# A four-stage Flamingo block on one core: output projection and routing by token halves, the first expert shares by a selector product, weights fetched during the attention, and key-query products behind the key tiles

## The reference, cut to what matters

```python
x = x + tanh(g_xattn[0]) * L0_xattn(layernorm(x), ctx)   # x (4, 256, 256), ctx (4, 1601, 128)
x = x + tanh(g_ffn[0])   * L0_ffn(layernorm(x))          # 32 experts of 96, top 8, capacity
x = x + tanh(g_xattn[1]) * L1_xattn(layernorm(x), ctx)   # 16 heads of 128, rms-normed q and k
x = x + tanh(g_ffn[1])   * L1_ffn(layernorm(x))          # 64 experts of 64, top 4, 2 shared
```

## Time and profile before

| | us |
|---|---|
| median of 3 runs | 1975.44 (1975.04 to 1980.54) |
| the profiled execution | 1977.05 |
| its span in the profile | 1974.9 |
| busy: TensorE / VectorE / ScalarE / GpSimd | 1829.2 / 1366.6 / 1162.3 / 336.6 |
| granted TensorE clock, mean over the span | 0.968 of full speed |

### The profile page before, as it was taken

The page is one execution under the profiler, slowest core; times in us unless marked ns, Lnnn a source line. Parts: engine busy times, 40 slices in busy tenths (PEclk is TensorE's granted clock), DMA queues, the critical chain, the costliest instruction groups (busy, mean ns, idle before and its releaser), DMA issues. The chain is left out here.

```text
span 1974.9 us, 31470 instructions
## 1 busy us (share of the span) xinstructions
PE 1829.2 (93%) x9085; PEld 1342.2 (68%) x9087; DVE 1366.6 (69%) x2268; ACT 1162.3 (59%) x1943; POOL 336.6 (17%) x298
## 2 busy tenths in 40 slices
PE   5789898949999889999899998999989998999998
PEld 3444444547888667776677766777667776788887
DVE  8565656245666678877778787878778786666665
ACT  2577666813333567776677767777667774333222
POOL 3010101023444300001000010000100002444442
PEclk9899999969999999999999999999999997999999
DMA  3413223155443200001000010000000001455553
GB/s 93 105 49 73 70 53 77 29 170 127 112 113 85 67 1 0 0 0 34 0 0 0 0 34 0 0 0 0 1 1 0 0 0 38 88 112 112 114 114 82
DMA packets 110127, 96.58 MB, mean 49 GB/s; under 512 B 72836, under 2 KB 94472, under 8 KB 109416
## 3 DMA queue, kind: packets, MB, share of 16 engines
q1 hardware_dynamic: 110056, 95.67, 19.7%
HBM read 73.73 MB, written 1.44 MB: 38 GB/s over the span
## 5 line engine op out<-in xcount | busy, mean ns | idle before, releaser
L902 ACT ACTIVATE s_p<-ps,s_g,s_rk 128x256 f32<-128x256 f32 (+1 forms) x832 | 412.3, 559 | 126.4 <-PE ps L1129 91.5
L1129 PE MATMUL ps<-s_qq,s_ctxT 128*128 (+2 forms) x1248 | 389.6, 425 | 18.4 <-ACT s_p L902 15.7
L423 PE MATMUL ps<-s_xT,s_wgus 128*128 128x512 f32 x1440 | 350.5, 393 | 3.0 <-DVE s_hw L1643 2.6
L423 PEld LDWEIGHTS ps<-s_xT,s_wgus 128*128 128x128 f32 x1440 | 272.2, 189 | 62.1 <-DVE s_hw L1643 3.4
L1129 PEld LDWEIGHTS ps<-s_qq,s_ctxT 128*128 128x128 f32 (+1 forms) x1248 | 231.7, 187 | 106.7 <-issue 47.2
L1129 PE MATMUL ps<-s_ps,s_ctx 128*128 128x512 f32 x960 | 276.5, 398 | 0.1
L817 ACT ACTIVATE s_p<-ps,s_bsm 128x1024 f32<-128x1024 f32 x208 | 219.1, 1111 | 96.1 <-PE ps L1010 85.0
L1763 DVE TENSOR_TENSOR s_dsum<-s_dsum,s_p 128x512 f32<-128x512 f32 (+1 forms) x352 | 242.2, 688 | 30.4 <-ACT s_p L902 19.6
L1772 DVE TENSOR_TENSOR s_ps<-s_p,s_ps 128x512 fp32r<-128x512 f32 x320 | 220.1, 688 | 13.2 <-ACT s_ps L908 9.8
L1129 PEld LDWEIGHTS ps<-s_ps,s_ctx 128*128 128x128 f32 x960 | 182.2, 190 | 46.7 <-DVE s_ps L1772 1.8
L1645 DVE TENSOR_TENSOR s_hs<-s_hw,s_hs 128x512 fp32r<-128x512 f32 x120 | 138.7, 1156 | 82.3 <-ACT s_hs L346 82.3
(11 more groups left out here) (253 smaller groups left out, 2128.5 us busy)
## 6 DMA issues: line engine op xcount, KB each, us to landing
s_wB<-w1s SPq DMA_DIRECT2D x64, 256.0 KB, 4.0
s_kT<-s_kst SPq DMA_DIRECT2D x96, 128.0 KB, 2.3
s_kT<-s_kst SPq DMA_DIRECT2D x96, 80.0 KB, 2.1
s_wB<-w0s SPq DMA_DIRECT2D x16, 384.0 KB, 3.8
s_wB<-w0s SPq DMA_DIRECT2D x16, 256.0 KB, 4.0
s_wgu<-in_L_ffn_Wg_dram SPq DMA_DIRECT2D x64, 64.0 KB, 3.0
s_wgu<-in_L_ffn_Wu_dram SPq DMA_DIRECT2D x64, 64.0 KB, 2.7
s_wd<-in_L_ffn_Wd_dram SPq DMA_DIRECT2D x64, 64.0 KB, 2.7
```

The costliest lines, as they stand in the source:

```text
L423: ins = nc.tensor.matmul(ps[:, 4 + g, :], wgus[:, slot, w, g, k, :], xT[:, x_, k, n], start=c == 0, stop=c == len(ops) - 1)
L902: ins = nc.scalar.activation(p1[0:r, SLOT1[t], j, :], ps[0:r, BANK1[t], j * SQ:(j + 1) * SQ], ACT.Exp, bias=g1[0:r, 3:4], scale=rk_col(t, ...
L1129: ins = nc.tensor.matmul(out, lhs(x_), rhs(y_), start=first and n == 0, stop=last and n == 2)
```

## The change

- The output bias is added to `x` (times the gate) during the last batch of the first attention, the tanh of the gates is taken before it, and the transposes of context tiles 0 to 3 are put into its visits 15 and 16.
- Output projection, update, normalization, transposes, logits, selection and counting are done for tokens 0 to 511 and then for 512 to 1023.
- Unit 0's shares aren't stored and loaded: two rows of them are multiplied with a selector (`unit_rows`), and VectorE copies the product to `wB`. The other units still go through memory.
- SyncE loads the weights of units 0 and 1 during the last batch, and the second attention's weights when the first half is projected. `gatew` is loaded at the start. GpSimd splits the first weights before the tokens.
- The third normalization's root table is loaded ahead of the m1 copies, and the root is taken after the fifth of them.
- In the second attention the first queries of a batch go to banks 4, 7, 5, 6, each with the wait for its own bank; the key-query products of the second token tile move from between the key tiles of quarter 3 to behind them.

The diff, cut to its core (helpers that only recount semaphores are left out):

```diff
+    if not more:
+        first.update({15: ("ctx", 0), 16: ("ctx", 1)})
...
# scalar
+            act_std(act, 1, slice(0, 4), 0)
+            act_take(act, 1, 0, (0, 1))
+            act_std(act, 1, slice(4, 8), 1)
+            act_split(act, 1, 0)
+            shares_exp(0)
+            act_take(act, 1, 1)
+            act_split(act, 1, 1)
+            shares_exp(1)
+            act.wait_ge(s.w_turned, 1)
+            nc.scalar.copy(wtf[0:E0, 0:HALF], ps[0:E0, 7, :]).then_inc(s.wT_ready, 1)
...
+            nc.scalar.activation(rq1[0:1, 1, 0:1], ones[0:1, 0:1], ACT.Sqrt).then_inc(s.act_steps, 1)
             for j in range(8):
+                if j == 5:
+                    act_std(act, 2)
...
+                split_products(TB * b + 1, 0)
                 act.wait_ge(s.k1_var, b + 1)
                 nc.scalar.activation(rk1[:], rk1[:], ACT.Sqrt).then_inc(s.k1_std, 1)
+                nc.scalar.activation(rq1[0:1, 1, 0:1], ones[0:1, 0:1], ACT.Exp).then_inc(s.act_steps, 1)
+                for j in range(1, 4):
+                    split_products(TB * b + 1, j)
                 act.wait_ge(s.rk1_ready, b + 1)
                 act.wait_ge(s.bound1_ready, 1)
 
-                nc.scalar.activation(rq1[0:1, 1, 0:1], ones[0:1, 0:1], ACT.Exp).then_inc(s.act_steps, 1)
...
# sync
-            sp.wait_ge(s.x_updated, 1)
-            load_router()
+            sp.wait_ge(s.misc_made, MISC["keys", B - 1, 1, 3] + 1)
+            sp.wait_ge(s.q_scaled, B)
             unit0(0, 0, None)
             unit0(0, 1, None)
 
+            sp.wait_ge(s.y0_made, 1)
...
-            store_shares(w0s, E0, 1)
-            shares0(0, 0, None)
+            store_shares(w0s, E0, 2, 1)
             shares0(0, 1, None)
...
# tensor
+            project_out((0,))
             turn_sums(B - 1, NG - 1)
+            project_out((1,))
             pe.wait_ge(s.ctx_made, NG * B)
+            for c in range(KD):
                 for t in range(4):
+                    nc.tensor.transpose(ps[:, 4 + c, t * P:(t + 1) * P], xn[:, 4 + t, c * P:(c + 1) * P], ident[:]).then_inc(s.cx_turned, 1)
+            project_out((2, 3)).then_inc(s.y0_made, 1)
+            pe.wait_ge(s.cxT_act, KD)
+            project_out(range(4, 8)).then_inc(s.y0_made, 1)
...
+            pe_turn_half(pe, 1, 0)
+            gate_logits(0)
+            pe_turn_half(pe, 1, 1)
+            gate_logits(1)
             pe.wait_ge(s.consts_made, 3)
+            positions(0)
             pe_zero(pe)
+            pe.wait_ge(s.xT_lo, 1)
+            pe_up(pe, 0, 0, 0, 1)
+            positions(1)
+            for half in range(2):
+                pe.wait_ge(s.w_ready, half + 1)
+                for t in range(4 * half, 4 * half + 4):
+                    ins = nc.tensor.transpose(ps[0:E0, 7 - half, (t % 4) * P:(t % 4 + 1) * P], rw[:, t, 0:E0], ident[:])
+                ins.then_inc(s.w_turned, 1)
+            pe.wait_ge(s.wT_ready, 2)
+            pe.wait_ge(s.rows_made, 1)
+            for half in range(2):
+                nc.tensor.matmul(ps[:, 7 - half, :], unit_rows[:], wtf[0:2, half * HALF:(half + 1) * HALF],
+                                 start=True, stop=True).then_inc(s.share_made, 1)
...
+                    if b and tt % TB == 0:
+                        pe.wait_ge((s.o1_read, s.den_read, s.y1_added, s.y1_added)[j], primed(8 * b))
...
-                if b:
-                    pe.wait_ge(s.y1_added, primed(8 * b))
-                    pe.wait_ge(s.o1_read, primed(8 * b))
...
-                    if q % 2 == 1 and 3 <= u < 7:
+                    if q == 1 and 3 <= u < 7:
+                        key_products(tt, u - 3)
...
+                for j in range(4):
+                    key_products(TB * b + 1, j)
                 pe.wait_ge(s.k1_squared, 4 * KT * (b + 1))
-                pe.wait_ge(s.qq_read, 4 * TB * (b + 1))
+                pe.wait_ge(s.qq_read, 4 * TB * b + 4 + 1)
...
# vector
+                    if not more and t == 6:
+                        add_bias()
+                    if not more and t >= 11:
+                        take_ctx(t - 11)
...
             for half in range(2):
+                dve.wait_ge(s.y0_made, half + 1)
+                update(ps[:, 2 * half:2 * half + 2, :].rearrange("p a n -> p (a n)"), 0, half, half)
+                normalize(1, range(4 * half, 4 * half + 4), half)
...
+            gates(0)
+            take_half(1, 1)
+            select(0)
+            gates(1)
+            admit(0)
+            select(1)
+            admit(1)
+            dve.wait_ge(s.w_turned, 2)
+            v.tensor_copy(wtf[0:E0, HALF:2 * HALF], ps[0:E0, 6, :]).then_inc(s.wT_ready, 1)
+            for half in range(2):
+                dve.wait_ge(s.share_made, half + 1)
+                v.tensor_copy(wB[:, 0, half * HALF:(half + 1) * HALF], ps[:, 7 - half, :]).then_inc(s.bslot0, 16)
...
                 v.tensor_scalar(rk1[:], rk1[:], 1.0 / D1, 1e-5, ALU.mult, ALU.add).then_inc(s.k1_var, 1)
+                low_products(TB * b + 1, 0)
                 dve.wait_ge(s.k1_std, b + 1)
                 v.reciprocal(rk1[:], rk1[:]).then_inc(s.rk1_ready, 1)
+                for j in range(1, 4):
+                    low_products(TB * b + 1, j)
```

More of the change, by code:

```diff
@@ L1053, in _, with project_out @@
                         values(b, step + k)
+            def project_out(tiles):
+                for t in tiles:
+                    for k in range(KD):
+                        ins = nc.tensor.matmul(ps[:, t // 2, (t % 2) * D:(t % 2 + 1) * D], xnT[:, k, t * P:(t + 1) * P],
+                                               wo0[:, k, :], start=k == 0, stop=k == KD - 1)
+                return ins
+            pe.wait_ge(s.small0_loaded, 16 * 3)
+            pe.wait_ge(s.misc_read, primed(MISC["ctx", 1] + 1))
@@ new lines, in positions @@
+            def positions(half):
+                pe.wait_ge(s.sel_ready, half + 1)
+                for t in range(4 * half, 4 * half + 4):
+                    nc.tensor.matmul(ps[:, 7 - half, t * E0:(t + 1) * E0], tri[:], selb[:, t, :], start=True, stop=False)
+                    ins = nc.tensor.matmul(ps[:, 7 - half, t * E0:(t + 1) * E0], onesb[:], pre[:, t, :], start=False, stop=True)
+                ins.then_inc(s.pos_made, 1)
+            pe.wait_ge(s.gate_loaded, 16)
+            pe_turn_half(pe, 1, 0)
@@ new lines, in select @@
+            def select(half):
+                tiles = range(4 * half, 4 * half + 4)
+                cols = slice(tiles[0], tiles[-1] + 1)
+                dve.wait_ge(s.r_exp, half + 1)
+                for t in tiles:
+                    me.did(v.max(m8[:, t, :], re[:, t, 0:E0]))
+                me.wait()
+                for t in tiles:
+                    me.did(v.match_replace(rr[:, t, 0:E0], m8[:, t, :], re[:, t, 0:E0], -1.0))
+                me.wait()
+                me.do(v.tensor_scalar(selb[:, cols, :], rr[:, cols, 0:E0], 0.0, None, ALU.is_lt))
+                if half == 0:
+                    me.do(v.tensor_scalar(pre[:, 0, :], selb[:, 0, :], 0.0, None, ALU.mult))
+                for t in tiles:
+                    if t:
+                        ins = v.tensor_tensor(pre[:, t, :], pre[:, t - 1, :], selb[:, t - 1, :], ALU.add)
+                        if t < tiles[-1]:
+                            me.do(ins)
+                ins.then_inc(s.sel_ready, 1)
+                me.do(v.tensor_tensor(rw[:, cols, 0:E0], re[:, cols, 0:E0], selb[:, cols, :], ALU.mult))
+                me.do(v.tensor_reduce(rsm[:, 1, cols], rw[:, cols, 0:E0], AX, ALU.add))
+                me.do(v.reciprocal(rsm[:, 2, cols], rsm[:, 1, cols]))
+                me.do(v.tensor_tensor(rw[:, cols, 0:E0], rw[:, cols, 0:E0], bc(rsm[:, 2, cols], E0), ALU.mult))
@@ L1789, in _ @@
             norm(3)
[L1790 to L1792 removed]
+            for half in range(2):
+                turned(dve, 3, half)
+            dve.wait_ge(s.router_loaded, 16 * 7)
             me.do(v.tensor_reduce(xm[:], xnT[:].rearrange("p k (b n) -> p (k b) n", b=B), AX, ALU.add))
```

283 lines of the change are left out of this document (139 added, 144 removed).

## The result

The changed kernel takes 1918.7 us (median of 4 runs, 1915.69 to 1920.38) against 1977.99 for the kernel before beside it: a ratio of 0.9692, 95% interval 0.9671 to 0.9713. The profiled execution took 1915.69, with a span of 1914.0 against 1974.9: 60.9 us less, where my sum had 52.7. The profiled execution is the fastest of the four (the others have spans of 1916.0 to 1918.7, at a mean clock of 0.980 or 0.981 instead of 0.984); by the medians the gain is 59.3.

A forecast was written before the change was run, and what follows sets the result against it. TensorE, busy 93% of the span, bounds the kernel; time lies where it waits for serial chains. 23.9 + 6.4 + 3 x 4.0 + 4 x 2.6 = 52.7 us off 1977.05, median 1.6 lower: 1923 us, range 1910 to 1938.

The forecast's parts named there:

- Place 1: From the first attention's last sums through routing to the first share multiplication and loop start: 23.9 us less.
- 22.4: Gain in us at Place 1 if GpSimd's port lock holds a VectorE selection step for up to 2.3 us.
- C: Rival: unit 1's shares come late through memory, 2 to 5 us lost once, 1925 to 1928 us; chance 0.13.
- E: Rival: SyncE paces the first expert loop and the kernel is slower, 1995 us at 3 us per unit; chance 0.03.
- Place 2: Before the second attention: earlier square root, transposes 3.2 us sooner, no low clock; 6.4 us less.
- Place 3: Start of second-attention batches 1 to 3: queries 2.2 us sooner and at high clock; 4.0 us less each.
- 8.83 becomes 6.9: Query products at the start of batches 1 to 3, in us, if without idle time the clock doesn't fall.
- Place 4: End of key tiles in all four second-attention batches: first exponential sooner by 2.6 us each.
- Rival D: A table switch costs 2.66 us, with a drain of 1.38 on top of the load: 1928 us; chance 0.10.
- rival B: Clock stays high: 4 us more at Place 1, up to 1.7 at each first exponential; 1912 us; chance 0.17.
- A: Rival: only the transitions gain, Place 3 and Place 4 give nothing; 30.3 us less, 1945 us; chance 0.08.
- F: Rival: nothing moves, a buffer wait makes Place 1 a serial chain again and the batches too; chance 0.01.

The follow-up runs named there:

- pool_late: Changed kernel, but GpSimd splits token half 0 only after VectorE normalized half 1, and half 1 only after the last shares are admitted; ratio 0.9700.
- place1_only: Changed kernel with the edits to the third normalization's root, the query banks and the moved key-query products all undone; ratio 0.9895.
- memory_shares: Changed kernel with only the selector product undone: unit 0's shares are stored by DMA and loaded back; ratio 0.9736.
- undo_heads: Changed kernel with query groups of batches 1 to 3 again in banks 4 to 7 behind the old two waits; ratio 0.9734.
- undo_products: Changed kernel with the last four groups of key-query products, their ScalarE copies and VectorE low parts back between the key tiles; ratio 0.9784.
- early_copy: Changed kernel with the second of four moved ScalarE copies, and its VectorE low part, ahead of the key root; ratio 0.9702.
- quiet_routing: Changed kernel with GpSimd's splits later and fifteen products of zeros on TensorE in the routing; ratio 0.9683.
- combined: Changed kernel with quiet_routing, early_copy and 31 products of zeros at the last transition together; median 1910.83 us, ratio 0.9661.
- products_busy: undo_products plus twelve products of zeros on TensorE while it waits for the first exponential; ratio 0.9762.
- undo_root: Changed kernel with the third normalization's root and its table load behind the eight m1 copies again; ratio 0.9726.

## Why the prediction was right, step by step

**The forecast is right in its places, and its closeness is partly luck.** The four places and their waits came as forecast; the sum was 8.2 us too small, mostly for want of one clock effect.

**Place 1: 23.9 forecast, 23.6 measured** (0.8 ahead of the last sums, 21.2 to the multiplication, 1.6 behind it; forecast -0.8, 22.9 and 1.8). The 0.8 at the attention's end isn't shown to be the change's, since that end scatters by 3.8. Two errors cancelled. Half 0 ran ahead of my times (its logits ended at 408.2, not 411.2), and VectorE lost two delays of 2.0, not one of 0.8. Both counted: the first held half 1's transposes back, the second the products that count places (TensorE waits 0.69 for them at 417.59), and the first up-product stands behind both; without the delays pool_late has the multiplication 2.75 sooner. Together the errors put that product, at low clock, where I had it: its end 424.0 for 424.1, the shares' copy 426.0 for 426.2. That is luck. The Trainium skill (SBUF — State Buffer, "Who interferes with whom") has the port pair locked for a whole instruction; the delayed instructions of three kernels end 0.03 to 0.15 behind GpSimd's (416.83 for 416.78), so the traces agree with it. Its 22.4 for this place was a little too low, though there were two such delays: half 0's lead made up for them. Of place 1's parts only the selector product was undone by itself; that the halves, the bias and the earlier weight loads give the rest, some 18 us, is read from the two traces, and place1_only confirms their sum alone.

**Selector product.** With it, 3.0 us lie between the shares' copy and the multiplication (426.0 to 429.0). The way through memory, 9.4 in the kernel before, takes 6.6 in memory_shares; the store's landing alone took 4.7 us before and 2.0 to 3.9 in the others. With 2.4 at the loop's start the product is worth 5.5. Unit 1's shares were in time: no multiplication in the loop waits for a DMA. Rivals C and E fall.

**Place 2: 6.4 forecast, 6.1 measured.** The transposes waited for the last m1 copy, the queries ran at full clock, the reduction waited for ScalarE.

**Place 3: 12.0 forecast, 10.0 measured** (2.2 for each wait and 1.7 twice, for the low clock in batches 1 and 3 of the kernel before; 8.2 by undo_heads, where the clock fell once; in place1_only it fell in all three). The mis-sized term is "8.83 becomes 6.9", which I took from batch 3 for all three; batch 2 had 7.13 all along.

**Place 4: 10.4 forecast, 13.4 measured.** The key root came where I put it (4.2 sooner). The three copies behind the load took 1.5, not 1.7, and the exponential starts 1.4 behind their start, in the third one's tail. The load took 1.28, and the next instruction started 0.02 behind it. Rival D, and with it the 1.38 us of drain that the Trainium skill (ScalarE: Activation LUTs, "What ACT_TABLE_LOAD costs") adds, falls as time on this path.

**What the sum lacked: the clock behind the first exponentials**, 14.6 - 10.0 = 4.6 in three batches and 1.1 in the last, 5.7 together (7.2 by undo_products). That is rival B's second half, "up to 1.7 more at each first exponential", which came true, while its first half (4 us at place 1) didn't. It was no independent chance but a consequence of my own place 4: 1.25 us of pause ahead of the exponential's products instead of 3.4 to 3.6. The 1.9 at the last transition is not the change's: the same instructions took 10.1 to 14.3 us there in the twelve kernels without fillers at that transition. A and F are out: places 3 and 4 gave 23.4.

In all, 52.7, less 0.6 at places 1 and 2, less 2.0 at place 3, plus 3.0 at place 4, 5.7 behind the first exponentials and 2.1 from the last transition on, makes the 60.9.

## What to carry to other kernels

Shortening a pause of TensorE pays twice where the pause used to drop its clock: price the products behind it at both clocks, and look at every repetition of the stage, not at one. Where the pause can't be shortened, products of zeros in it are a cheap remedy: they were worth 7 us over four batches here. At the last transition they took 3.5 us, of which 0.7 to 0.9 came back in the stage behind, and in the routing nine of them gave nothing that could be told from scatter; fifteen together with GpSimd's later splits gave 3.0. Before a stall is removed, look for what ends next: early_copy took 0.5 us from ScalarE and gained 0.24, and pool_late had the multiplication 2.75 us sooner and kept 0.2 of it at the loop's end. And before a gain of one us is read from one trace, look at the same interval in kernels that don't touch it: here that interval alone scatters by 1.1.

## What the runs showed of the hardware

The same idle time (1.95 us) ahead of the same sixteen products was followed by the high clock in two batches and the low one in the third of one execution. VectorE steps of 0.17 and 0.29 us, and one of four tensor-scalar steps, took 1.8 to 2.0 us longer while GpSimd ran a 128x1024 subtraction; VectorE copies out of PSUM under such an instruction (0.68 at 421.72 in pool_late) and the searches for maxima (0.46 for four at 409.42 in quiet_routing, GpSimd from 408.62 to 410.98) did not. With the routing shortened, the low clock came back in the first steps of the expert loop for 6.8 us, at a cost of 2.6 us in pool_late and quiet_routing and of 1.0 in combined; but in four kernels with the routing as it is (products_busy, undo_heads, undo_root, place1_only) it came back there for 3.4 us, at 0.5 to 1.0. What ties the two is open.
